# A two-layer graph-attention kernel: VectorE instead of GpSimd finishes the second layer's chunks

## What is computed

```
# layer 0 (leaky slope 0.2, keys and values are entity_embs), then x = layernorm(x + elu(out + x))
# layer 1 (leaky slope 0.01, keys and values are x @ W), then x = layernorm(x + out + bias)
e   = s[:, None] + t[None, :]            # s, t: one score for each row and each column
e   = leaky_relu(e)
e   = where(adj > 0, e, -big)
out = softmax(e, axis=1) @ values
```

## Time and profile before

| | |
|---|---|
| median of three runs | 630.98 us (630.66 to 631.12) |
| the profiled execution | 630.16 us, of which the span of the core's instructions is 628.3 us |
| chunk 6, from its first L1100 to that of chunk 7 | 409.04 to 471.51 us |
| chunk 7 | 471.51 to 534.00 us |
| chunk 8 | 534.00 to 591.15 us |
| chunk 9, to the end of its last L1100 | 591.15 to 617.30 us |
| busy in the span | PE 80%, DVE 89%, ACT 86%, POOL 26% |

### The profile page before, as it was taken

One profiled execution on the slowest core, in us unless ns is written; L12 is line 12 of the kernel. 1 busy time (PEld: TensorE's weight loads), 2 busy tenths in 40 slices (PEclk: granted clock), 3 DMA queues, 4 the chain that ended last, 5 costly groups with the idle time before them and its releaser, 6 DMA issues.

```text
span 628.3 us, 14305 instructions
## 1 busy us (share of the span) xinstructions
PE 504.9 (80%) x6039; PEld 234.8 (37%) x6039; DVE 559.5 (89%) x781; ACT 541.7 (86%) x627; POOL 163.1 (26%) x105
## 2 busy tenths in 40 slices
PE   1317776989989799999989776788798888899994
PEld 1214444434444334434445443343333333333352
DVE  5999999999899998989978979869998998889795
ACT  1879995889999998899989889988896999679883
POOL 1171000366026650177002001005401520221050
PEclk9999888889999999999999999989999999999997
DMA  8999984866567656460100010000000000000000
GB/s 200 386 380 344 341 321 163 275 226 238 203 232 270 230 174 237 152 210 1 27 28 2 2 35 1 35 2 2 9 33 2 1 18 18 2 1 18 2 18 9
DMA packets 21340, 76.16 MB, mean 121 GB/s; under 512 B 10412, under 2 KB 11612, under 8 KB 13084
## 3 DMA queue, kind: packets, MB, share of 16 engines
q1 hardware_dynamic: 20472, 74.89, 34.4%
q0 software_dynamic: 112, 0.28, 0.1%
q10 hardware_dynamic: 692, 0.08, 0.1%
HBM read 74.16 MB, written 1.09 MB: 120 GB/s over the span
## 4 chain that ended last, share of the span: by engine, by line
issue 30%; DVE 25%; ACT 20%; PE 18%; DMA 3%; POOL 2%; POOLq 0%; SPq 0%; ACTq 0%; DVEq 0%
ACT Pm L810 14%; DVE junk L942 13%; PE acc L1221 10%; DVE zps L1100 5%; PE zps L1282 5%; DMA adj_in<-in_adj 3%; DVE v L919 2%; ACT zps L802 2%; ACT v L668 2%; PE acc L1228 2%; DMA VE<-in_L_gnn_entity_embs 1%; PE zps L1191 1%; ACT u_row L684 1%; POOL tAB L547 0%; DVE tot L1006 0%
## 5 line engine op out<-in xcount | busy, mean ns | idle before, releaser
L810 ACT ACTIVATE Pm<-zps,ebias 128x1024 f32<-128x1024 f32 (+1 forms) x320 | 292.0, 933 | 43.6 <-DVE zps L1100 37.9
L802 ACT ACTIVATE zps<-S_row,ntau_col 128x1024 f32<-128x1024 f32 (+1 forms) x211 | 200.6, 954 | 5.7
L1282 PE MATMUL zps<-D,v 128*128 128x128 bf16 x2048 | 164.8, 224 | 36.5 <-ACT zps L802 22.8
L1282 PEld LDWEIGHTS zps<-D,v 128*128 128x128 fp8e4 x2048 | 118.8, 99 | 176.8 <-ACT zps L802 86.4
L1221 PE MATMUL acc<-Pm,VE 128*32 128x512 f32 (+2 forms) x1280 | 147.8, 535 | 21.4 <-ACT Pm L810 14.4
L1221 PE MATMUL acc<-Pm,X 128*32 128x512 f32 (+2 forms) x1280 | 140.1, 524 | 27.8 <-ACT Pm L810 24.1
L942 DVE CUSTOM_DVE_ANT_0 junk<-v,u_row 128x2048 int8<-128x2048 int8 x64 | 155.4, 2441 | 0.2
L942 DVE CUSTOM_DVE_ANT_0 junk<-v,adj_in 128x2048 int8<-128x2048 int8 (+3 forms) x88 | 154.6, 1795 | 0.0
L1100 DVE SCALAR_TENSOR_TENSOR zps<-S_row,tau_col,zps 128x1024 f32<-128x1024 f32 (+1 forms) x109 | 112.7, 1055 | 41.0 <-PE zps L1282 40.4
L1228 PE MATMUL acc<-Pm,ones 128*32 128x256 f32 (+1 forms) x1280 | 87.5, 346 | 0.0
L1228 PEld LDWEIGHTS acc<-Pm,ones 128*32 128x32 f32 x1280 | 42.8, 113 | 72.2 <-issue 62.1
(11 more groups left out here) (170 smaller groups left out, 250.0 us busy)
## 6 DMA issues: line engine op xcount, KB each, us to landing
adj_in<-in_adj SPq DMA_DIRECT2D x62, 1024.0 KB, 6.5
S_row<-S_rows_scratch SPq DMA_DIRECT2D x6, 512.0 KB, 4.1
Pm<-in_adj SPq DMA_DIRECT2D x2, 1024.0 KB, 10.5
VE<-in_L_gnn_entity_embs SPq DMA_DIRECT2D x2, 512.0 KB, 5.8
S_row<-S_rows_scratch SPq DMA_DIRECT2D x3, 256.0 KB, 3.1
out<-tAB SPq DMA_DIRECT2D x3, 256.0 KB, 2.6
adj_in<-u_row_scratch SPq DMA_DIRECT2D x2, 256.0 KB, 3.5
S_row<-S_rows_scratch POOLq DMA_DIRECT2D x1, 256.0 KB, 7.3
```

What stands on the lines that cost most here:

```text
L802: a.activation(mask_of(n), S_row[:, C % 2, 0:R(C) * P], ACT.Relu, bias=ntau_col[:, layer(C), n % JT:n % JT + 1]).then_inc(seed_done, 1)
L810: a.activation(Pm_of(k, 0, R(C) * P), mask_of(k), ACT.Exp, bias=ebias[:, layer(C), int(seeded(k)), J:J + 1])\
L1282: last = t.matmul(mask[:, r * P:(r + 1) * P], v[:, chunks[C][1] + r, J * P:(J + 1) * P], D[:, C % 2, PART * second + r, :], start=(r * P % ...
```

## The change

The set of chunks that VectorE finishes grows from 3, 4 and 9 to 3 to 9, so that chunks 5, 6, 7 and 8 move from GpSimd to VectorE, all but the power. In the VectorE loop `add_up` (with `reciprocal` in it) runs at J = 9, `normalise` (with `sums` and `squares` in it) at J = 13, and `scale` at J = 18. The seeds of chunks 7 and 8 become 21 and 12. The unseeded steps of chunk 7 are then 0, 1, 2, 3, 5, 8, 12, 16, 20, 24, 28, and the seeded ones of chunk 8 are 6, 8, 10, 13, 15, 17, 20, 22, 24, 27, 29, 31. Chunk 6 keeps 20 seeds.

```diff
-SEEDS = ((29, 28, 28, 26, 24), (28, 20, 20, 10, 0))
+SEEDS = ((29, 28, 28, 26, 24), (28, 20, 21, 12, 0))
...
-    IN_LAYER_1 = dict(reciprocal=7, sums=13, squares=18)
+    IN_LAYER_1 = dict(add_up=9, normalise=13, scale=18)
...
-    BY_VECTOR = (NC - 2, NC - 1, LAST)
+    BY_VECTOR = (NC - 2, *range(NC - 1, NCH))
...
                         if J == at("normalise", C):
                             normalise(dve, d, link, C - 1, sums, squares)
+                        if J == at("scale", C):
+                            scale(dve, d, C - 1)
```

## The result

| | before | after |
|---|---|---|
| median of four runs | 630.82 us (629.87 to 631.12) | 642.88 us (642.22 to 644.97) |
| the profiled execution | 630.16 us | 642.7 us |
| its span | 628.3 us | 640.9 us |

What follows compares the result with a forecast made beforehand. VectorE was taken as busiest (89%) and nearly full in the last chunk, with ScalarE pacing chunk 7 and TensorE chunk 8. 2.0 + 2.7 + 0.4 + 4.5 = 9.6 us on the median 630.98 gave 640.6 us, range 633.5 to 644.

Steps and rivals of the forecast that it cites:

- Chunk 6: VectorE's moved work at steps 9 and 13 delays the exponential of step 15; +2.0 us, bounds 1.0 and 2.5.
- Chunk 7: A gain of 0.76 us at step 5, then ScalarE waits for VectorE; +2.7 us, bounds 1 and 3.5.
- the three waits: In chunk 7 ScalarE waits for VectorE 2.0 us at step 12, 1.3 at step 16 and 0.8 at step 20.
- the order costs and not the load: In chunk 7 VectorE's load hardly changes (+0.4 us); three blocks of 3 us ahead of a mask addition cost.
- The walk through steps 8, 12, 16 and 20: In chunk 7, VectorE's work against ScalarE's between mask additions: 8.8 against 7.5 us to step 16; 4.1 us of waits.
- Chunk 8: TensorE paces: start 0.8 us earlier, new waits 4.35, old 3.5 gone, a fourth of a clock dip; +0.4, bounds -1, +3.
- Chunk 9: In the last chunk all 5.05 us lands where VectorE idles only 0.6; +4.5 us, bounds 4.0 and 5.2.
- the sign that VectorE has no idle time up to the last addition: Last chunk: VectorE idle 0 from the fifth L1100 to the last, that stretch 26.3 instead of 21.8 us.
- Absorbed: Rival, chance 0.14: blocks cost nothing in chunks 6 and 7, 8 gains up to 1 us, 9 pays 4.5; 634.5 us.
- The returned port: Rival, chance 0.11: maxima freed of contention and filled idle time make chunks 6 to 8 6.7 us shorter; 628.8 us.
- The clock: Rival, chance 0.05: TensorE falls to 0.50 behind three new waits in chunks 7 and 8, 1.6 us each; 645 us.
- The power: Rival given no chance: `scale` at J = 18 has to wait for GpSimd's power, so VectorE stalls.

Runs made afterwards that it cites:

- the kernel with the wide chunks alone: The kernel before with chunks 5, 6 and 7 finished by VectorE, chunk 8 by GpSimd as before, seeds 20, 21, 12; 638.66 us, ratio 1.0119.
- the thin kernel: The kernel before with GpSimd's layer 1 instructions for chunks 5 to 8 covering one feature of 64, the power taking a constant; 624.62 us, ratio 0.9899.

## Why the prediction was right, and where a term was off

The sign, the place and three of the four mechanisms held; the sum, 9.6 us, was 3.0 short of the 12.6 in the trace, and the time, 642.88, lies in the range, 2.3 us above the forecast. There is some luck in that: a third spell of 1.5 us where TensorE paces would have been enough to leave the range, and one of the four executions, 644.97, does.

*Chunk 6.* +2.0 forecast, +2.10 measured, and as much in the kernel with the wide chunks alone. I had put all of it on the exponential of step 15; 1.16 us came there (3.41 less the 2.25 of the earlier trace rows) and 0.90 before it (1.18 more at step 9, 0.28 less at step 12). What the one takes on of the delay the other doesn't have to, so the sum held.

*Chunk 7.* +2.7 forecast, +2.65 measured, with the three waits nearly to the tenth. The seed of step 7 cost nothing, as forecast: ScalarE's wait at step 5 was shorter by the 0.76 and by the seed. One part of the reasoning was wrong and hardly showed. The sentence that the order costs and not the load fell: single pieces at the same steps leave the chunk at 64.89. The walk through steps 8, 12, 16 and 20 was right because it counted VectorE's load against ScalarE's between two additions. Its summary ("VectorE's whole load hardly changes") compared loads over the whole chunk, of which only the part up to step 20 counts. There each us is paid, by the comparison with the thin kernel: 4.19 for the 3.85, by estimate, that VectorE has more.

*Chunk 8*, the step that failed: +0.4 forecast, +2.30 measured. Between the products of steps 4 and 28 lie 43.78 us, which is 37.2 of TensorE's own pace and 6.6 of waits and slow clock, where 3.5 were before. From step 4 to 14 it is 19.98 us, 4.5 more than ten steps at 1.549: the wait of 2.77 (3.1 forecast) and 1.7 more, of which five small waits show 1.3 (1.25 forecast). From step 14 to 28 it is 23.80, 2.1 more than fourteen steps: 1.5 of clock (the first two steps take 4.63 us in the place of 3.10), of which the sum held 0.4, and 0.6 of small waits that it didn't hold. So the mis-sized term is the clock: I took a fourth of a dip behind the 2.77 us wait, though the earlier trace rows had shown a whole one behind a wait of 2.04. The old dip was counted as gone (it is part of the 3.5) and only a fourth of a new one put in its place: that made the chunk look nearly free.

*Chunk 9.* +4.5 forecast, +5.83 measured. The load term is right: the last chunk alone, with no slow clock, pays 4.26. The other 1.57 is the clock again, at a place where I had not looked for it: the product waits 2.48 us for what is behind `normalise`, and TensorE goes on at 0.50. Behind the same wait the clock stays up in the kernel that moves the last chunk alone and in that with the old seeds, so this term comes or doesn't. This also refutes the sign that VectorE has no idle time up to the last addition: after 622.21 TensorE paces, and of the 27.66 us of that stretch 1.46 are idle.

*The rivals.* "Absorbed" fell with the waits in chunks 6 and 7. "The returned port" is true as a mechanism, 5.2 us off the maxima, and 4.9 us of time at an equal clock in the kernel with thin GpSimd work, of the 6.7 that the rival counted on (its 1.43 for L555 included), and loses on the balance, because the moved work costs more than it frees: at an equal clock 16.2 us against 4.9. "The clock" (645) was the nearest rival: two costly spells in the place of one, rather than three; a further one in chunk 7 came as the rival said, but cost nothing there. The power held nothing up at steps 13 and 18.

*What stays open.* Why TensorE's clock falls behind one wait and not behind another of the same length, or even behind the same one. In the kernel before it fell behind the wait of 2.04 us in chunk 8 and stayed at 1.00 behind a longer one in chunk 7, as TensorE in time and its clock by stretches show:

```profile
486.13 1.07 PE L1221 MATMUL acc<-Pm,X 128*32 128x512 f32 x8 [2.30 <-ACT Pm L810]
```

```profile
485.00:487.00 2.00, 0.87 (x8) 1.00 0.00 0
487.00:489.00 2.00, 1.50 (x20) 1.00 0.00 0
```

In the kernel with the square four times it stayed up behind the very wait of step 4 in chunk 8:

```profile
549.86 1.06 PE L1223 MATMUL acc<-Pm,X 128*32 128x512 f32 x8 [2.04 <-ACT Pm L812]
```

```profile
550.00:552.00 2.00, 2.00 (x24) 1.00 0.00 0
```

The median of the changed kernel with the old seeds is 1.6 us lower, in keeping with two spells less, yet that the seeds cause it was not shown.

## What to carry to other kernels

Price moved work in the part of the stage where it lands: where the target engine is full and the next engine waits for it, each us is paid nearly in full, however idle the engine is at the stage's end, and the same work in single pieces up to that end can cost much less (here 0.4 us in the place of 4.2 in chunk 7, 2.9 for 4.65 in chunk 6). A slower engine that runs beside should keep work wherever it shares nothing with the saturated one (here the last chunk), and may give it up where it holds that engine up (here beside the maxima), if there is idle time to put it in; that this is a gain at an equal clock was not shown here. The clock may be lower behind every new wait of TensorE, and the runs don't say in advance whether it will: count it in full or not at all, never as a fraction, give both sums, and look for such waits in each stage where TensorE paces.

## What the runs showed of the hardware

- A spell of TensorE at the granted clock of 0.50, the 1.2 GHz level, came behind waits of 2.04, 2.48 and 2.77 us in chunks 8 and 9, and stayed away behind waits of 2.04, 2.30, 2.49 and 2.87 us (the last in chunk 8 of the kernel with the old seeds). It costs about 1.5 us where TensorE paces (chunk 8 is 57.15 in the kernel before, with one, and 55.67 in that with the square four times, without) and nothing where ScalarE or VectorE does (chunk 6: 62.47 with one, 62.48 without).
- GpSimd's instructions over 512 floats take 1.04 us by themselves, the residual (L564) 1.28 and beside a maximum 3.30; the maximum beside it goes from 2.28 to as much as 3.36. In chunk 9 before, where there are no maxima:

```profile
598.38 1.04 POOL L559 TENSOR_TENSOR o<-o,rden 128x512 f32<-128x512 f32 x1 [0.60 <-DVE rden L591]
599.50 1.28 POOL L564 TENSOR_TENSOR tAB<-o,X 128x512 f32<-128x512 f32 x1
```

  Each of these takes VectorE 0.69. The Trainium skill ("GPSIMD Engine Reference", 4.1 Engine selection) gives such elementwise work to VectorE, as GpSimd is about 2x slower with two inputs: by the duration alone the trace agrees in the direction, with 1.5x for L559 and 1.9x for L564. But in the last chunk 7 instructions that take GpSimd longer cost the kernel nothing there, and 4.3 us or more on VectorE: here the measured time of the whole decides against the table.
- Lost busy time isn't lost time. The maxima give back 5.2 us of busy time. With GpSimd's work thinned out the kernel is 6.5 us faster, of which 1.5 is a spell of the clock and 1.4 the wait for L555; what is left, about 3.5 us, is by this sum the time that the contention cost.
